# Causal mask of the third attention as triangles on quarters of TensorE, and its TensorE program without a loop

## The chip, the cores and the metric

The kernel runs on one core of one Trainium2 chip. The metric is the device time of one execution in microseconds (us). Three runs of the kernel before took 2063.49, 2064.55 and 2067.57 us, median 2064.55. Engines are TensorE (PE; its weight loads are PEld), VectorE (DVE), ScalarE (ACT), GpSimd (POOL) and SyncE, which issues the transfers (SPq).

## The reference

The reference is a stack of four layers on x of 16 samples x 256 tokens x 256 features, each an attention and a feed-forward part with a modulated layer norm in front and a gate behind: eight stages. The change touches the third stage, the attention of layer 1 (differential attention with 16 heads of two maps each, so 32 maps with 8 features):

```python
q = (x @ Wq).reshape(b, t, 2 * H, HD).transpose(0, 2, 1, 3) * scaling     # H = 16, HD = 8
k = (x @ Wk).reshape(b, t, 2 * H, HD).transpose(0, 2, 1, 3)
v = (x @ Wv).reshape(b, t, H, 2 * HD).transpose(0, 2, 1, 3)
scores = jnp.einsum('bhqd,bhkd->bhqk', q, k)
causal = jnp.triu(jnp.full((t, t), -jnp.inf, dtype=jnp.float32), 1)
aw = jax.nn.softmax((scores + causal).astype(jnp.float32), axis=-1)
aw = aw.reshape(b, H, 2, t, t)
aw = aw[:, :, 0] - lam * aw[:, :, 1]
attn = jnp.einsum('bhqk,bhkd->bhqd', aw, v)
attn = attn * jax.lax.rsqrt(jnp.mean(attn * attn, axis=-1, keepdims=True) + 1e-05)
attn = attn * (1.0 - LAMBDA_INIT)
return attn.transpose(0, 2, 1, 3).reshape(b, t, H * 2 * HD) @ Wo
```

## The kernel before

All of x stays in SBUF. Each engine has its own program, written by hand stage by stage (`l1a_tensor`, `l1a_vector`, `l1a_scalar`, `l1a_pool` and the `l1a_..._sync` functions for the third stage), and they meet by semaphores only. A stage's program is a function `slot(i)`, one per sample, called by the helper `slots`: some slots written out, the steady ones in a loop of two slots per turn (even and odd samples use different buffers), the last ones written out. For the third stage the loop covers slots 4 to 11 (`LOOP2`) on TensorE, VectorE, ScalarE and GpSimd. In the loop a semaphore's target is computed in a register.

In one slot TensorE interleaves three samples: the score maxima of sample i, most exponentials and the values of sample i - 1, the output of sample i - 2, and the projections of sample i + 1. The order is the one in `slot`.

Scores are computed twice. q and k are split in three bf16 parts each, and their products are six terms of eight features, 48 rows (`M_ROW`), stacked in QS and KS. `max_pair` computes scores with queries on the partitions, 48 rows deep, for two maps at once: map pr = 0 on rows 0 to 63 of the array, pr = 1 on rows 64 to 127, each into its own PSUM bank. VectorE takes the negated maximum over the keys (`maxima`, line 2322), GpSimd splits it in three bf16 parts, TensorE transposes them (`max_T`, line 2022), ScalarE copies them (`maxT`, line 2226) and SyncE writes them into QS (`l1a_max_sync`, line 2500), three rows behind the 48, against ones in KS. `exp_pair` then computes the scores again with keys on the partitions over 64 rows, now with the maximum taken off, and ScalarE takes the exponential straight from PSUM (line 2237). `values` multiplies by v (lines 2084, 2086), four heads on four 32-column tiles of the array.

A bank holds 512 columns. For each group of four heads (o = 0 to 3) there are three pairs (n = 0 to 2). Two of the three, here called short masks, hold two heads with 256 columns each, of which 128 need the mask; the third, the long mask, holds four heads with 128 columns, all masked (queries and keys of the same 128 tokens). The mask is a matmul too: the identity `ident_b` as weights over the whole array, a table of 0 and -1e30 (`later4` for the maxima, `earlier4` for the exponentials) as moving data. For short masks it comes behind the data (lines 2015, 2060), for long ones ahead of them (lines 2001, 2064). A sample has 24 pairs, 16 with a short and 8 with a long mask. Three banks turn round for the maxima and three for the exponentials: a pair waits until VectorE (`s.max`) or ScalarE (`s.prob`) has read the banks that it writes.

Work on the whole array (128 rows), on halves (64 rows, two side by side) and on 32-column tiles are three configurations of the array. The projections, transposes and masks use the whole one.

## Time and profile before

| | |
|---|---|
| median of the runs | 2064.55 us |
| profiled execution | 2068.32 us |
| its span, first to last instruction | 2066.5 us |
| TensorE busy, share of the span | 1837.7 us, 89% |
| VectorE | 1374.8 us, 67% |
| GpSimd | 901.9 us, 44% |
| ScalarE | 740.8 us, 36% |
| mean granted TensorE clock | 0.952 |
| chain that ended last, shares | TensorE 68%, VectorE 19%, issue 6% |

The third attention lies between 664.3 us (its first score matmul) and about 1226 us. TensorE's busy time is modelled: matmuls overlap in the array, so start-to-start distances are read rather than durations. A row with a bracket says how long the engine was idle ahead of it and what released it. Some matmul records are missing (a row x1 where two stand in the program).

### The profile page before, as it was taken

To read this page: it belongs to the slowest core of one execution; us is meant where nothing else is said; L and a number is where in the kernel's file an instruction comes from. 1 tells how busy PE (TensorE), PEld (TensorE's weight loads), DVE (VectorE), ACT (ScalarE), POOL (GpSimd) and SP (SyncE) were. 2 spreads that over 40 slices of the span, in tenths; PEclk is the share of its full clock that TensorE was granted. 3 is DMA by queue.
4 is the path that set the end of the run, shared out by engine and by line. 5 is a ranking of instruction groups with operands and counts; after the bars stand their busy time and mean duration, and the time that the engine had idled before them with its cause. 6 is when DMAs were issued, how large, how long until landed. Compare 5 with 4: busy or idle time off the path is not lost.

```text
span 2066.5 us, 39950 instructions
## 1 busy us (share of the span) xinstructions
PE 1837.7 (89%) x13335; PEld 1266.3 (61%) x13400; DVE 1374.8 (67%) x3587; ACT 740.8 (36%) x1511; POOL 901.9 (44%) x965
## 2 busy tenths in 40 slices
PE   8999999689997899999999988899867788998887
PEld 5555555489996455555555446677655667885443
DVE  4677767465554656565656567888846776886775
ACT  2544444122222464656464541111122223443332
POOL 0354545465555254545454443333343224663333
PEclk9999999799999899999999999999999888999787
DMA  5300000100004646454545400000011000000011
GB/s 181 106 6 8 5 8 6 35 6 10 9 10 95 138 84 112 84 109 81 109 81 111 79 7 14 8 10 8 15 32 41 13 16 16 16 13 18 31 38 41
DMA packets 68177, 93.34 MB, mean 45 GB/s; under 512 B 9852, under 2 KB 62316, under 8 KB 64748
## 3 DMA queue, kind: packets, MB, share of 16 engines
q1 hardware_dynamic: 68076, 92.01, 19.6%
q8 instruction: 61, 1.00, 0.2%
q14 instruction: 40, 0.33, 0.1%
HBM read 61.70 MB, written 29.49 MB: 44 GB/s over the span
## 4 chain that ended last, share of the span: by engine, by line
PE 68%; DVE 19%; issue 6%; POOL 2%; ACT 2%; DMA 1%; DVEq 1%; SPq 0%; POOLq 0%; ACTq 0%
PE PS L1029 16%; PE PS L2084 3%; PE PS L677 3%; DVE negmax L2322 3%; PE PS L1960 3%; PE PS L1196 3%; PE PS L734 3%; PE PS L750 2%; PE PS L510 2%; PE PS L2012 2%; DVE xn L500 2%; PE PS L2015 2%; PE PS L731 2%; PE PS L2057 2%; PE PS L701 1%
## 5 line engine op out<-in xcount | busy, mean ns | idle before, releaser
L2322 DVE TENSOR_REDUCE negmax<-PS 128x2 f32<-128x512 f32 (+1 forms) x384 | 247.1, 685 | 191.6 <-PE PS L2015 98.0
L541 POOL TENSOR_TENSOR X<-X,y_sb 128x512 f32 (+1 forms) x128 | 165.2, 1291 | 147.7 <-DVE y_sb L536 142.7
L536 DVE TENSOR_TENSOR y_sb<-PS,ga_sb 128x512 f32<-128x512 f32 x96 | 66.2, 690 | 180.3 <-PE PS L1029 50.4
L1029 PE MATMUL PS<-we_hi,h_parts 128*128 128x512 f32 x512 | 177.7, 407 | 1.6 <-POOL h_parts L1478 1.5
L500 DVE TENSOR_SCALAR xn<-X,mv,rs 128x256 f32 (+1 forms) x256 | 155.6, 649 | 22.5 <-POOL rs L493 21.2
L520 ACT ACTIVATE hT<-PS,modT 128x256 f32<-128x256 f32 x256 | 130.0, 559 | 112.5 <-PE PS L510 111.6
L2237 ACT ACTIVATE pw<-PS 128x512 f32<-128x512 f32 x256 | 139.0, 600 | 75.0 <-PE PS L2060 75.0
L491 POOL TENSOR_TENSOR rs<-mv,eps 128x2 f32<-128x2 f32 x128 | 26.6, 208 | 293.4 <-DVE mv L484 293.2
L1029 PE MATMUL PS<-l_h_parts,lut_hi 128*128 128x256 f32 (+1 forms) x768 | 145.7, 291 | 6.7 <-POOL l_h_parts L1162 6.7
L1029 PEld LDWEIGHTS PS<-l_h_parts,lut_hi 128*128 128x128 f32 (+1 forms) x768 | 117.8, 184 | 9.7 <-issue 5.4
L1572 DVE SCALAR_TENSOR_TENSOR l_acc<-PS,rt_g,l_acc 128x256 f32<-128x256 f32 x256 | 105.8, 475 | 20.8 <-PE PS L1029 20.7
L1029 PEld LDWEIGHTS PS<-we_hi,h_parts 128*128 128x128 f32 x512 | 96.8, 189 | 27.5 <-issue 7.1
L1029 PE MATMUL PS<-l_h_parts,lut_lo 128*128 128x256 f32 (+1 forms) x384 | 110.2, 287 | 0.0
L510 PE MATMUL PS<-ident,xn 128*128 128x128 f32 x512 | 82.1, 284 | 30.6 <-DVE xn L500 30.6
L1029 PE MATMUL PS<-we_lo,h_parts 128*128 128x512 f32 x256 | 101.9, 398 | 0.0
L1101 ACT ACTIVATE l0f_act<-PS 128x256 f32<-128x256 f32 x96 | 36.8, 383 | 176.4 <-PE PS L1029 176.4
L1196 PE MATMUL PS<-hT,l_wqkv 128*128 128x256 f32 x384 | 94.8, 399 | 5.1 <-ACT hT L520 4.3
L493 POOL TENSOR_TENSOR rs<-rs,half 128x2 f32<-128x2 f32 x128 | 94.1, 735 | 10.0
L1171 POOL TENSOR_TENSOR l0f_hid_parts<-l0f_hid,l0f_hid_parts 128x256 fp32r<-128x256 f32 x96 | 72.3, 754 | 53.2 <-DVE l0f_hid_parts L1023 52.7
L479 DVE BATCH_NORM_STATS2 st<-X 128x6 f32 (+1 forms) x256 | 95.1, 413 | 0.3
L510 PEld LDWEIGHTS PS<-ident,xn 128*128 128x128 f32 x512 | 58.7, 143 | 55.8 <-DVE xn L500 38.3
L997 POOL TENSOR_TENSOR l_ms<-l_ms,half 128x32 f32<-128x32 f32 x16 | 87.1, 5442 | 1.3
(279 smaller groups left out, 4372.3 us busy)
## 6 DMA issues: line engine op xcount, KB each, us to landing
ga_sb<-ga_dram SPq DMA_DIRECT2D x128, 128.0 KB, 2.9
qk_dram<-qk_parts SPq DMA_DIRECT2D x64, 192.0 KB, 2.8
KS<-qk_dram SPq DMA_DIRECT2D x32, 384.0 KB, 5.9
QS<-qk_dram SPq DMA_DIRECT2D x32, 384.0 KB, 9.3
qk_dram<-qk_parts SPq DMA_DIRECT2D x64, 128.0 KB, 2.8
wmod<-in_wmod SPq DMA_DIRECT2D x4, 1536.0 KB, 13.6
qk_dram<-qk_parts SPq DMA_DIRECT2D x64, 64.0 KB, 2.5
y_out<-X SPq DMA_DIRECT2D x16, 256.0 KB, 2.2
```

Source lines behind the costliest of these rows:

```text
L479: last_ = dve.bn_stats(st6[b.par][:, t, :], xb(b)[:, t, :])
L493: pool.tensor_tensor(rs[b.par][:, :], rs[b.par][:, :], half[:, 0:TT], ALU.pow).then_inc(s.rstd.sem, 1)
L500: last_ = dve.tensor_scalar(xn[b.par][:, t, :], xb(b)[:, t, :], mv[b.par][:, t, 0:1], rs[b.par][:, t:t + 1], ALU.subtract, ALU.mult)
L510: last_ = pe.transpose(PS[:, 0, kh * T + t * P:kh * T + (t + 1) * P], xn[b.par][:, t, kh * P:(kh + 1) * P], ident[:, :])
L520: last_ = act.activation(hT[b.par][:, kh, :], PS[:, 0, kh * T:(kh + 1) * T], ACT.Identity, bias=modT[:, sub, 0, kh, bass.ds(b.n, 1)], scal ...
L541: pool.tensor_tensor(xb(b), xb(b), y_sb[b.par][:, :, :], ALU.add).then_inc(s.x.sem, 1)
L997: pool.tensor_tensor(ms_sb[:, :], ms_sb[:, :], half[:, 0:TT * HEADS], ALU.pow).then_inc(s.rn.sem, 1)
L1029: last_ = pe.matmul(out, x.bitcast(F32R), y.bitcast(F32R), start=start and n == 0, stop=stop and n == 2)
L1196: last_ = pe.matmul(bank(1 + n)[:, m * T:(m + 1) * T], l3_wqkv[:, kh, n * D + m * P:n * D + (m + 1) * P], hT[b.par][:, kh, :], start=kh == ...
L1572: dve.scalar_tensor_tensor(l1_acc[b.par][:, t, :], bank(1 + (2 * q + t) % 4)[:, e * D:(e + 1) * D], rt_g[b.par][:, t, x_:x_ + 1], l1_acc[b ...
L2237: act.activation(to.rearrange("p a n -> p (a n)"), bank(4 + (2 * n + pr) % 3), ACT.Exp).then_inc(s.prob.sem, 1)
L2322: dve.tensor_reduce(to, src, AX.X, ALU.max, negate=True).then_inc(s.max.sem, 1)
```

## The change

Three things change, all for the third stage.

1. The mask. The upper right 128x128 mask splits in a 64x64 square that is masked altogether and two 64x64 triangles on the diagonal. The square goes into the data matmuls: two more rows in QS and KS (`S_ROW` is the old 48, `M_ROW` now 50), one per tile of 128 tokens, with 1 in the first 64 queries of the tile and -1e30 in its last 64 keys (`cut`). The triangles are added by `triangles`, four matmuls per pair with weights and data of 64x64: rows and columns 0 to 63 or 64 to 127 of the array, for bank 0 and bank 1 in turn. They now come behind the data in all pairs, and signal both banks in the second round.
2. `slots` can go without a loop, and TensorE's program of this stage is written out for all samples. The other engines keep their loop.
3. `l1a_cut_sync`: eight transfers that write the two rows, in the second stage (L0_ffn) at sample 14, and a wait for them at the start of TensorE's third stage.

```diff
 def slots(eng, slot, first, steady, last):
 
+    if steady is None:
+        steady = (first + first % 2,) * 2
     lo, hi = steady
-    assert lo % 2 == 0 and hi % 2 == 0 and hi > lo
+    assert lo % 2 == 0 and hi % 2 == 0 and hi >= lo
     for i in range(first, lo):
         slot(Idx(None, i))
-    with eng.Fori(lo // 2, hi // 2) as r:
-        slot(Idx(r * 2, 0))
-        slot(Idx(r * 2, 1))
+    if hi > lo:
+        with eng.Fori(lo // 2, hi // 2) as r:
+            slot(Idx(r * 2, 0))
+            slot(Idx(r * 2, 1))
...
+    cut_q, cut_k = np.zeros((2, HEADS, T), f), np.zeros((2, HEADS, T), f)
+    for t in range(TT):
+        cut_q[t, :, t * P:t * P + P // 2] = 1
+        cut_k[t, :, t * P + P // 2:(t + 1) * P] = LOW
+    out["cut"] = np.stack([cut_q, cut_k]).astype(bf)
...
+            pe.wait_ge(setup["a_pad"], 16 * 8)
...
+            def triangles(banks, tri, n, done):
+                for half_ in range(2):
+                    for pr in range(2):
+                        h = pr ^ half_
+                        r0, r1 = 64 * h, 64 * h + 64
+                        last_ = pe.matmul(banks[pr][r0:r1, :, r0:r1], ident_b[r0:r1, r0:r1], tri[r0:r1, 0:n, r0:r1],
+                                          start=False, stop=True)
+                        if half_ == 1:
+                            last_.then_inc(done.sem, 1)
...
                 if n == 0:
-                    for pr in range(2):
-                        pe.matmul(banks[pr], ident_b[:, :], later4[:, :, :], start=True, stop=False)
                     for j in range(4):
                         for pr in range(2):
-                            last_ = pe.matmul(banks[pr][:, j * P:(j + 1) * P], half_rows(q, pr, 4 * o + j, 0, P, M_ROW),
-                                              half_rows(k, pr, 4 * o + j, 0, P, M_ROW), start=False, stop=j == 3)
-                            if j == 3:
-                                last_.then_inc(s.max_ps.sem, 1)
+                            pe.matmul(banks[pr][:, j * P:(j + 1) * P], half_rows(q, pr, 4 * o + j, 0, P, M_ROW),
+                                      half_rows(k, pr, 4 * o + j, 0, P, M_ROW), start=j == 0, stop=False)
+                    triangles([x.rearrange("p (j k) -> p j k", j=4) for x in banks], later4, 4, s.max_ps)
                 else:
...
-                    for pr in range(2):
-                        pe.matmul(banks[pr].rearrange("p (j k) -> p j k", j=2)[:, :, P:T], ident_b[:, :], later4[:, 0:2, :],
-                                  start=False, stop=True).then_inc(s.max_ps.sem, 1)
+                    triangles([x.rearrange("p (j k) -> p j k", j=2)[:, :, P:T] for x in banks], later4, 2, s.max_ps)
...
-            slots(pe, slot, -2, LOOP2, B if pl + 1 < len(sigs) else B + 1)
+            slots(pe, slot, -2, None, B if pl + 1 < len(sigs) else B + 1)
...
-        M_ROW = 8 * N_TERMS
+        S_ROW = 8 * N_TERMS
+        M_ROW = S_ROW + TT
+
+
+        def l1a_cut_sync(sp):
+            sp.wait_ge(setup["a_zero"], 4)
+            for i in range(2):
+                for c, to in enumerate((QS, KS)):
+                    for r in range(2):
+                        sp.dma_start(to[i][64 * r + S_ROW:64 * r + M_ROW, :, :], ins["cut"][c]).then_inc(setup["a_pad"], 16)
...
-                    to = (QS, KS)[c][i.par][64 * r:64 * r + M_ROW, :, :].rearrange("p g t -> p (g t)")
+                    to = (QS, KS)[c][i.par][64 * r:64 * r + S_ROW, :, :].rearrange("p g t -> p (g t)")
...
+                    if i.reg is None and i.off == B - 2 and p == 1:
+                        l1a_cut_sync(sp)
```

`exp_pair` changes in the same way, with `earlier4`.

How TensorE's order moves is seen at the turn from one slot to the next, where it goes from the exponentials of one sample to the maxima of another, with the projection of k (`l_wk`) behind. Names are out<-moving data, weights, and the shape is that of the output. Before, outside the loop:

```order
L2057 MATMUL PS<-QS,KS 128x256 x4
L2060 MATMUL PS<-earlier,ident_b 128x2x128 x2
L2001 MATMUL PS<-later,ident_b 128x512 x2
L2004 MATMUL PS<-KS,QS 128x128 x8
L2064 MATMUL PS<-earlier,ident_b 128x512 x2
L2067 MATMUL PS<-QS,KS 128x128 x8
L1960 MATMUL PS<-hT,l_wk 128x256 x4
L2057 MATMUL PS<-QS,KS 128x256 x4
L2060 MATMUL PS<-earlier,ident_b 128x2x128 x2
L2012 MATMUL PS<-KS,QS 128x256 x4
L2015 MATMUL PS<-later,ident_b 128x2x128 x2
```

The same place of the changed kernel, with its own line numbers (2005 is `triangles`):

```order
L2073 MATMUL PS<-QS,KS 128x256 x4
L2005 MATMUL PS<-earlier,ident_b 64x2x64 x4
L2023 MATMUL PS<-KS,QS 128x128 x8
L2005 MATMUL PS<-later,ident_b 64x4x64 x4
L2079 MATMUL PS<-QS,KS 128x128 x8
L2005 MATMUL PS<-earlier,ident_b 64x4x64 x4
L1969 MATMUL PS<-hT,l_wk 128x256 x4
L2073 MATMUL PS<-QS,KS 128x256 x4
L2005 MATMUL PS<-earlier,ident_b 64x2x64 x4
L2030 MATMUL PS<-KS,QS 128x256 x4
L2005 MATMUL PS<-later,ident_b 64x2x64 x4
```

The long masks (512 columns, ahead of the data) stood next to other whole-array work and are now four triangles each behind the data. Short masks keep their place and become four triangles too.

In the loop of before TensorE's rows at the same turn have register instructions between them:

```order
L132 UNCONDITIONAL_BRANCH
L132 ISA
L1997 ISA
L2001 MATMUL PS<-later,ident_b 128x512 x2
L2004 MATMUL PS<-KS,QS 128x128 x8
L2045 REGISTER_ALU
L2064 MATMUL PS<-earlier,ident_b 128x512 x2
L2067 MATMUL PS<-QS,KS 128x128 x8
L1965 REGISTER_ALU
L1967 REGISTER_ALU
L1960 MATMUL PS<-hT,l_wk 128x256 x4
```

In the changed kernel this stage has none of them on TensorE. The last piece is SyncE's, at the end of the second stage: the gate loads of its samples 14 and 15, with the transfers of the two rows between, and the first transfer of the third stage. The changed kernel:

```order
L536 DMA ga_sb<-ga_dram 128x256
L2485 DMA QS<-in_cut 2x4096 x2
L2485 DMA KS<-in_cut 2x4096 x2
L2485 DMA QS<-in_cut 2x4096 x2
L2485 DMA KS<-in_cut 2x4096 x2
L536 DMA ga_sb<-ga_dram 128x256
L2496 DMA qk_dram<-qk_parts 64x3x512
```

The rows of `in_cut` stand there once for each of the two buffers; before, the two gate loads followed each other.

## Rows read from the trace of the kernel before

**Rows 1.** Busy us per stretch: from:to, length, PE, PEld, DVE, ACT, POOL, PEclk, DMA share, GB/s.

```profile
690.00:1190.00 500.00, 471.39 (x5148) 266.73 (x5206) 308.20 (x603) 279.44 (x547) 243.29 (x277) 1.00 0.51 99
748.36:783.17 34.81, 33.05 (x362) 18.85 (x365) 21.82 (x43) 19.39 (x38) 17.57 (x20) 1.00 0.52 95
817.98:852.78 34.80, 33.05 (x362) 18.85 (x365) 21.82 (x43) 19.47 (x38) 17.49 (x20) 1.00 0.53 100
```

**Rows 2.** TensorE in order of time: start us, length us, line, out<-in, rows*columns of the array.

```profile
836.00 0.39 PE L2057 MATMUL PS<-QS,KS 64*128 64x256 bf16 x4
836.32 0.39 PE L2060 MATMUL PS<-earlier,ident_b 128*128 128x256 bf16 x2
836.65 0.39 PE L2012 MATMUL PS<-KS,QS 48*128 48x256 bf16 x4
...
840.41 0.39 PE L2060 MATMUL PS<-earlier,ident_b 128*128 128x256 bf16 x2
840.64 0.59 PE L2001 MATMUL PS<-later,ident_b 128*128 128x512 bf16 x2
841.17 0.40 PE L2004 MATMUL PS<-KS,QS 48*128 48x128 bf16 x8
```

**Rows 3.** TensorE in order of time, eighth stage: 8, 64 and 72 columns.

```profile
1886.79 1.03 PE L1765 MATMUL PS<-hT,l_m 128*8 128x256 f32 x4
1887.75 1.08 PE L1719 MATMUL PS<-hT,l_sw 128*64 128x256 f32 x4
1888.76 1.08 PE L1721 MATMUL PS<-hT,l_up 128*72 128x256 f32 x4
```

**Rows 4.** TensorE in order of time, second stage: from 128 to 48 columns.

```profile
618.99 0.28 PE L1029 MATMUL PS<-l_h_parts,lut_lo 128*128 128x256 f32 x1
619.11 0.40 PE L1029 MATMUL PS<-l_h_parts,lut_hi 128*48 128x256 f32 x2
```

**Rows 5.** Groups by line: busy us, mean ns of one, idle us before; weight load of 64 columns.

```profile
L1719 PEld LDWEIGHTS PS<-hT,l_sw 128*64 128x64 f32 x64 | 7.7, 142 | 13.1 <-issue 8.1 <-DVE l_c L1815 2.0 <-ACT hT L520 0.4
```

**Rows 6.** Weight loads in order of time, first stage: strips of 32 rows.

```profile
208.56 0.31 PEld L731 LDWEIGHTS PS<-l_qT,l_kT 32*128 32x128 f32 x8 [0.33 <-issue]
```

**Rows 7.** Waits of SyncE's queue, 440 to 640 us: us in total, times, longest.

```profile
SPq L528 <- DVE y_sb L536: 182.2, 13, 21.7
```

**Rows 8.** TensorE in order of time, with its waits for VectorE.

```profile
848.91 0.39 PE L2012 MATMUL PS<-KS,QS 48*128 48x256 bf16 x4
...
850.30 0.39 PE L2012 MATMUL PS<-KS,QS 48*128 48x256 bf16 x4 [0.68 <-DVE negmax L2322]
...
859.40 0.39 PE L2012 MATMUL PS<-KS,QS 48*128 48x256 bf16 x4 [0.32 <-DVE negmax L2322]
```

**Rows 9.** VectorE in order of time.

```profile
858.66 2.67 DVE L2322 TENSOR_REDUCE negmax<-PS 128x2 f32<-128x512 f32 x4
```

**Rows 10.** ScalarE in order of time.

```profile
836.64 1.08 ACT L2237 ACTIVATE pw<-PS 128x512 f32<-128x512 f32 x2
```

**Rows 11.** TensorE in order of time: transpose of the maxima, and their use.

```profile
863.65 0.28 PE L2022 MATMUL PS<-ident_b,mparts 128*128 128x128 bf16 x2
...
868.07 0.39 PE L2057 MATMUL PS<-QS,KS 64*128 64x256 bf16 x4
```

**Rows 12.** TensorE in order of time, the same in the last sample.

```profile
1176.93 0.29 PE L2022 MATMUL PS<-ident_b,mparts 128*128 128x128 bf16 x2
...
1181.03 0.39 PE L2057 MATMUL PS<-QS,KS 64*128 64x256 bf16 x4 [1.54 <-DMA QS<-maxT]
...
1182.65 1.08 PE L2084 MATMUL PS<-pw,l_vpad 128*32 128x256 f32 x8
...
1185.34 0.39 PE L2057 MATMUL PS<-QS,KS 64*128 64x256 bf16 x4
```

**Rows 13.** Transfers issued from 829 to 864 us: KB each, median us to landing.

```profile
QS<-qk_dram SPq DMA_DIRECT2D x2, 384.0 KB, 9.9
```

**Rows 14.** SyncE's queue in order of time.

```profile
852.35 0.88 SPq L2489 DMA_DIRECT2D QS<-qk_dram  x2
```

More of the change, by code:

```diff
@@ L2058, in exp_pair @@
                                       half_rows(q, pr, g, 0, T, 64), start=j == 0, stop=False)
-                    for pr in range(2):
-                        pe.matmul(banks[pr].rearrange("p (j q) -> p j q", j=2)[:, :, 0:P], ident_b[:, :], earlier4[:, 0:2, :],
-                                  start=False, stop=True).then_inc(s.score.sem, 1)
-                else:
-                    for pr in range(2):
-                        pe.matmul(banks[pr], ident_b[:, :], earlier4[:, :, :], start=True, stop=False)
+                    triangles([x.rearrange("p (j q) -> p j q", j=2)[:, :, 0:P] for x in banks], earlier4, 2, s.score)
+                else:
                     for j in range(4):
                         for pr in range(2):
-                            last_ = pe.matmul(banks[pr][:, j * P:(j + 1) * P], half_rows(k, pr, 4 * o + j, P, T, 64),
-                                              half_rows(q, pr, 4 * o + j, P, T, 64), start=False, stop=j == 3)
-                            if j == 3:
-                                last_.then_inc(s.score.sem, 1)
+                            pe.matmul(banks[pr][:, j * P:(j + 1) * P], half_rows(k, pr, 4 * o + j, P, T, 64),
+                                      half_rows(q, pr, 4 * o + j, P, T, 64), start=j == 0, stop=False)
+                    triangles([x.rearrange("p (j q) -> p j q", j=4) for x in banks], earlier4, 4, s.score)
             def values(b, o):
```

## The prediction

> **What bounds the kernel now.** I read the stages first (busy time of each engine in stretches), then the order of time inside the third attention, the one stage that is changed, then who waits there. In the 500 us of its steady part TensorE is busy 471 us at the full clock, VectorE 308, ScalarE 279, GpSimd 243, and the DMA engines half of the time [rows 1]. Cut at ScalarE's eviction of the values, which comes once a sample, a sample takes 34.8 us [rows 1]. So the stage is TensorE's, with short stretches in which it waits for another engine.
>
> **What a mask costs.** A score pair is some data matmuls on two halves of the array (64 rows each, side by side) and a mask on the whole array. From start to start the four data matmuls of 256 columns take 0.32 us (836.00 to 836.32), the two masks of 256 columns 0.33 (836.32 to 836.65), and the two masks of 512 columns 0.53 (840.64 to 841.17) [rows 2]. So 512 more mask columns cost 0.21, two masks of 256 stream for 0.21, and 0.11 is left: the price of going from whole array to halves. Halves to whole costs the same (0.32 less two rounds of 0.107). Where a whole-array mask follows whole-array work there is no such price: 840.41 to 840.64 is 0.23 [rows 2].
>
> **The change, part by part.**
> (a) Stream. The mask of 128x128 becomes four triangles of 64x64: two rounds of 128 columns for the short mask (0.107 us in place of 0.213), two rounds of 256 for the long one (0.213 in place of 0.427), if the quarters run side by side as the halves do. A sample has 16 short and 8 long masks: 16 x 0.107 + 8 x 0.213 = 3.4 us.
> (b) Switches. The long mask came first, often right behind whole-array work, as the order rows show. Now each of the 24 pairs is halves, then quarters. Changes of configuration counted through one sample: 50 before, 60 now; 10 x 0.11 = 1.1 us more, if halves to quarters costs 0.11 too. No row has this switch. The nearest keep all rows and change the columns: from 8 to 64 columns costs 1887.75 - 1886.79 - 4 x 0.213 = 0.11, from 64 to 72 columns 0.16 [rows 3]; 128 to 48 columns costs nothing, as the step of 0.12 stays (618.99 to 619.11) [rows 4]. Bounds 0 and 0.16; I take 0.11, the row whose matmuls end at 64 columns. The Trainium skill (TensorEngine Tiling (Array Packing), Tiling Modes, Key Properties) says that changing the tiling mode, unlike changing the tile, drains TensorE: a rule against this change. By it all 60 cost, and the sum is mine; the row at 619.11 does not agree, and by that row the 24 inner ones are free, which is rival 1.
> (c) Weights. Each triangle loads 64 columns of the identity: four loads where there were two. A load of 64 columns in f32 lasts 142 ns [rows 5]; I take no more for bf16. Loads overlap where they go to different rows: eight, to four row strips, stand in 0.31 us [rows 6], where even one of half its columns lasts 0.14. The triangles go to two different halves of the rows, so I take no cost; the other bound is that each load holds up the next, which makes a short mask as long as before (rival 3). The Trainium skill (TensorE: Matmul & The Clock Gate, Part 2) gives the quick weight load to 128 columns only and otherwise P / 1.2 ns for P columns: an estimate of 53 ns, four in a row 0.21, which would be rival 3. No row here has a bf16 load of 64 columns.
> (d) The data matmuls of the maxima get two more rows (48 to 50) and no more columns, and those of the exponentials always had 64 rows at the same 0.32. Nothing.
> (e) The program without the loop. One sample stands outside the loop (748.36 to 783.17), one in it (817.98 to 852.78): 34.81 and 34.80 us, TensorE busy 33.05 in both [rows 1]. So the loop costs nothing now, and writing it out gives nothing. Below zero: more code to fetch, which the sample outside had too. Above: register instructions before waits could begin to count once pairs are shorter, and are gone.
> (f) Eight small transfers on SyncE's queue, late in the second stage, at about 0.44 us of issue each (0.88 for two, [rows 14]): 3.5 us, ahead of one gate load. That queue waits 182 us for VectorE there, over 13 loads [rows 7]. Hidden; without that cover one gate load would be 3.5 us late, once.
>
> **What TensorE gets to keep.** Its work falls by 3.4 - 1.1 = 2.3 us a sample, but in six stretches another engine sets the length.
> VectorE, three times. From 848.91 to 850.30, 1.39 us, are data, switch, one mask, a maximum of 0.69 and the hand-over: none gets shorter, since the first of two masks in a row was as long as two rounds of triangles [rows 8]. The stretch before it (L2012 at 845.00) has the same 1.39. And up to 859.40, from the last transpose to tokens on, VectorE runs without a pause (its maxima from 858.66 on have no idle time ahead), and TensorE waits 0.32 for it [rows 8, 9]. These hold 5 short masks and 1 of the new switches.
> ScalarE, three times. The pair that starts at 836.00 has its first exponential at 836.64, which ends 0.6 later; with the hand-over the next exponential pair cannot start before 1.3 us have gone [rows 10]. TensorE's own two pairs there take 2 x 0.65 now, 2 x 0.54 after. The same holds seven microseconds later, and behind the transpose at 863.65, where two evictions stand ahead on ScalarE. These hold 5 short masks, 1 long, 3 new switches.
> Left: 6 x 0.107 + 7 x 0.213 = 2.13 us, less 6 x 0.11 = 0.66: 1.47.
> Then a new wait. The negated maxima go through a transpose on TensorE, ScalarE, and SyncE's transfer, before the third group's exponentials. TensorE has 863.65 to 868.07, 4.42 us, between transpose and use [rows 11]; in the last sample, where a projection between them is missing, it waited 1.54 us and used them 4.10 after (1176.93 to 1181.03) [rows 12]. After: 4.42 - 0.53 + 0.11 = 4.0, a wait of 0.1; behind it in TensorE's order stands everything. The big loads of Q and K land 9.9 us after their issue at 852.35 to 853.23, by 863.1, and are used from about 864.4; that comes 1.3 earlier at most, and their own issue moves too: nothing [rows 13, 14].
> Kept: 1.47 - 0.1 = 1.35 us a sample. The steady part from 683 to 1181 us is 14.3 samples: 19 us. The first sample (maxima alone, VectorE's) and the last (exponentials alone, ScalarE's) give nothing.
> The profiled execution took 2068.3 us for a span of 2066.5; less 19 it is 2049. The median of the runs shown lies 3.8 lower, at 2064.55: I forecast 2046.
>
> **Rivals.**
> 1. Halves to quarters is free. For it the row at 619.11, against it [rows 3]. The 13 pairs outside the set stretches gain 0.11 more each, 1.4 us: 2.75 a sample, 39 us, 2025.
> 2. Slower: the quarters don't run side by side, in all 24 masks of a sample. The triangles stream 0.213 and 0.427 as before, the 6 switches (0.66) stay as pure cost, and in the VectorE and ScalarE stretches the banks come up to 0.1 later: 0.9 more a sample, 13 us, 2077. It decides once a short mask streams over 0.17. For it: no row has two tiles that differ in rows and columns both; against: halves do run side by side.
> 3. The four weight loads follow one another: a short mask stays 0.21, a long one gets 0.21. 7 x 0.213 = 1.49, less 0.66, less 0.1 for the maxima, less 0.5 in the set stretches, where both masks come 0.1 later: 0.2 a sample, 3 us, 2062. Against it [rows 6].
> 4. Behind the wait of 1.54 the clock was low, and the values took 2.69 us (1182.65 to 1185.34) [rows 12], half of which they need at the full clock. If the new waits did this in each sample, 1.3 would eat the gain: 2064. Against it: waits of 0.68 in each sample leave the clock at 1.00 [rows 1, 8].
> That the change doesn't do what it says can only be its second half, and (e) says that.
>
> **Chances and range.** Forecast 0.50, rival 1 0.16, rival 2 0.12, rival 3 0.12, rival 4 0.04, something unnamed 0.06 spread over all. A measurement of this kernel tells about 0.2%, 4 us, from no change. Faster 0.73 (forecast, rival 1, a part of rival 3), same 0.13, slower 0.14. The forecast's own range, with the switch at 0.09 to 0.13, is 2036 to 2054. To 2024 the range takes in rival 1, to 2070 rivals 3 and 4 and the near part of 2.
>
> **What would show it.** The sample's 34.81 us become 33.3 to 33.6. From the first short triangle to the next data matmul 0.22 (0.32: loads one after another, or not side by side); from data to triangles 0.32 (0.21: the switch is free). TensorE still waits for VectorE at three places, longest at the third; a wait of about 0.1 for the maxima's transfer and waits for ScalarE before exponential pairs appear. Clock 1.00 from 690 to 1170. The forecast is wrong if the sample's step is over 34.2 or under 32.8, or if another stage moves by more than 3 us.

## The result, and the profile after

The changed kernel takes 2040.46 us (median of 4 runs, 2036.71 to 2046.87), the kernel before 2064.02 (median of 4, 2063.12 to 2067.57). The ratio is 0.9882, with a 95% interval of 0.9862 to 0.9901: faster by 23.6 us. The forecast was 2046, in a range of 2024 to 2070.

The stage that is changed, in the trace after: busy us per stretch, in the columns of [rows 1].

```profile
804.93:838.40 33.47, 31.48 (x414) 19.09 (x413) 21.93 (x43) 19.51 (x38) 17.48 (x20) 1.00 0.51 101
690.00:1160.00 470.00, 438.01 (x5774) 264.74 (x5776) 307.18 (x598) 272.96 (x533) 240.76 (x275) 1.00 0.53 104
```

A sample takes 33.47 us where it took 34.81, with the clock at 1.00. TensorE is busy 1.6 us less than the 33.05 of [rows 1], with 52 more matmul records: 48 triangles, and 4 that the trace of before lacks. Against the complete records of the same masks (33.47, shown below for the kernel before without its loop) it is 2.0 us less, where 2.3 were forecast. The other three engines do what they did.

TensorE in order of time in the same trace: start us, length us, line, out<-in, rows*columns of the array.

```profile
848.88 0.28 PE L2038 MATMUL PS<-ident_b,mparts 128*128 128x128 bf16 x2
849.10 0.39 PE L2073 MATMUL PS<-QS,KS 64*128 64x256 bf16 x4
849.42 0.30 PE L2005 MATMUL PS<-earlier,ident_b 64*64 64x128 bf16 x4
849.66 0.40 PE L2023 MATMUL PS<-KS,QS 50*128 50x128 bf16 x8
849.98 0.41 PE L2005 MATMUL PS<-later,ident_b 64*64 64x256 bf16 x4
850.49 0.40 PE L2079 MATMUL PS<-QS,KS 64*128 64x128 bf16 x8
850.82 0.41 PE L2005 MATMUL PS<-earlier,ident_b 64*64 64x256 bf16 x4
851.15 1.99 PE L1969 MATMUL PS<-hT,l_wk 128*128 128x256 f32 x8
853.08 0.39 PE L2073 MATMUL PS<-QS,KS 64*128 64x256 bf16 x4
```

Data to triangles is 0.32 (849.10 to 849.42), of which 0.21 is stream; a short mask to the next data 0.24; a long mask to the next matmuls 0.33 (850.82 to 851.15), about 0.10 more than the short one for 512 more columns spread over four matmuls. What TensorE waited for in the sample from 804.93 to 838.40 (total us, times, longest), first its matmuls, then its weight loads:

```profile
PE PS L2030 <- DVE negmax L2333: 1.2, 2, 0.8
PE PS L2023 <- DVE negmax L2333: 0.2, 1, 0.2
```

```profile
PEld PS L2079 <- ACT pw L2248: 1.0, 3, 0.4
PEld PS L2073 <- ACT pw L2248: 0.5, 2, 0.3
PEld PS L2073 <- ACT pz L2248: 0.3, 1, 0.3
```

VectorE holds TensorE's matmuls at three places, and ScalarE its weight loads at six.

**Where the time came from.** GpSimd adds to x once a sample, 16 times a stage. I compare the stretch between its thirteenth addition of the second stage and its first of the fourth, which holds the third stage and a little of both neighbours. These two additions in the trace after:

```profile
605.68 1.30 POOL L549 TENSOR_TENSOR X<-X,y_sb 128x512 f32 x1 [2.94 <-DVE y_sb L544]
1232.90 1.30 POOL L549 TENSOR_TENSOR X<-X,y_sb 128x512 f32<-128x512 f32 x1
```

That is 627.2 us, and 651.4 in the kernel before (612.66 to 1264.02): 24.1 less. From the last addition of the second stage to the last of the third it is 575.3 (645.34 to 1220.61) and 599.4 (652.29 to 1251.70), again 24.1 less. Twelve steady samples give 16.2 (401.54 us against 417.70 between the same evictions), the two samples ahead of them 2.0 and 1.4, and the end of the stage 4.6. In the profiled executions 7.5 us more went elsewhere, 6.2 of them in the first 90 us, where the code is the same: the same 32 small matmuls took 7.01 us in one execution and 4.05 in the other. The median moved by 23.6, close to the stage's 24.1, so those 7.5 are put down to the two executions and not to the change.

### The profile page after: what moved, and what is told of

It reads as the page before. It is cut to its first block, busy times and chain, and to the rows that moved or that the text cites. A ratio compares the mean times of both kernels' runs of the same rounds, so it can differ in the third digit from the quotient of the medians.

```text
span 2034.9 us, 41282 instructions
## 1 busy us (share of the span) xinstructions
PE 1804.3 (89%) x14168; PEld 1264.1 (62%) x14168; DVE 1374.9 (68%) x3587; ACT 742.3 (36%) x1511; POOL 902.2 (44%) x965
## 4 chain that ended last, share of the span: by engine, by line
PE 64%; DVE 20%; issue 7%; ACT 4%; POOL 2%; DMA 1%; DVEq 1%; SPq 0%; ACTq 0%; POOLq 0%
PE PS L1037 16%; PE PS L2005 4%; PE PS L685 3%; PE PS L742 3%; DVE negmax L2333 3%; PE PS L1969 3%; PE PS L1204 3%; PE PS L2095 3%; PE PS L758 2%; DVE xn L508 2%; PE PS L518 2%; PE PS L739 2%; ACT pw L2248 2%; PE PS L2030 2%; PE PS L709 2%
```

## The experiments

All are compared by the steady step (one sample, from eviction to eviction, as in [rows 1]) and by the length of the third stage, which in the table is the stretch between additions as just defined. Both are read inside one execution, so what differs at its head doesn't enter. A single execution's whole time varies by 5 us and more, and the kernel before, run beside each group of experiments, took 2061.1 to 2066.5.

| kernel | steady step | third stage | whole |
|---|---|---|---|
| before | 34.81 | 651.4 | 2064.0 |
| before, TensorE's loop written out | 34.80 | 651.4 | 2061.8 |
| before, loop, masks cut in two | 35.17, three of 43 | 679.6 | 2096.6 |
| changed | 33.47 | 627.2 | 2040.5 |
| changed, with the loop | 33.47, three of 42 | 655.8 | 2062.8 |
| triangles in the exponentials alone, loop | 34.03 | 639.2 | 2052.5 |
| triangles, one quarter a round | 33.53 | 636.2 | 2045.7 |
| triangles, one row half | 33.46 and 34.83 | 649.4 | 2064.6 |
| triangles, one quarter only | 35.88 | 679.9 | 2090.5 |
| whole masks on halves | 33.61 | 632.4 | 2045.9 |
| triangles on halves | 31.39 | 599.8 | 2010.5 |
| no triangles | 30.7 mean | 587.7 | 2001.1 |

The whole times of the changed kernel, of the kernel before and of triangles on halves are medians; all else is one execution each. The step is the median of the twelve steady samples, where the table gives one number and no mean. The stage's length also holds its start and end, where the clock goes to its lower level for a longer or a shorter time: in the kernel before 34.1 us in all, in the changed one 30.7, with one quarter a round 51.2. A difference of a few us in the stage that the steady samples don't show therefore tells nothing by itself.

### The two halves of the change, each alone

The changed kernel with TensorE's loop put back:

```diff
-            slots(pe, slot, -2, None, B if pl + 1 < len(sigs) else B + 1)
+            slots(pe, slot, -2, LOOP2, B if pl + 1 < len(sigs) else B + 1)
```

> The changed kernel with TensorE's loop over pairs of samples put back; the triangles stay. Compared by the steady step of the third stage (ScalarE's eviction of the values, once a sample), 33.47 us in the changed kernel. My theory: the loop costs nothing, so 33.4 to 33.5 in the samples of the loop too, and TensorE's waits stay as they are. Rival: with shorter pairs the register instructions of the loop begin to count: over 33.6 inside the loop, and 33.47 only in the samples outside it.

Measured: both theories were wrong. The ordinary samples take 33.47, but three take 41.67, 41.77 and 41.39: every second one between 836 and 1028 us, and the loop of samples 4 to 11 goes back three times. One ordinary sample and one of the three, in the columns of [rows 1]:

```profile
802.88:836.35 33.47, 31.48 (x414) 19.09 (x413) 21.94 (x43) 19.51 (x38) 17.48 (x20) 1.00 0.51 98
836.35:878.02 41.67, 33.88 (x414) 20.47 (x413) 21.89 (x43) 19.51 (x38) 17.52 (x20) 0.92 0.44 85
```

TensorE has two long gaps in the long sample, both put down to "issue": no semaphore and no engine that the trace knows held it. In order of time:

```profile
847.38 0.30 PE L2005 MATMUL PS<-earlier,ident_b 64*64 64x128 bf16 x4
850.51 0.40 PE L2023 MATMUL PS<-KS,QS 50*128 50x128 bf16 x8 [2.83 <-issue]
850.84 0.41 PE L2005 MATMUL PS<-later,ident_b 64*64 64x256 bf16 x3
854.31 0.42 PE L2005 MATMUL PS<-later,ident_b 64*64 64x256 bf16 x1 [3.07 <-issue]
```

And the stretch around the second one and behind it:

```profile
852.00:859.00 7.00, 4.69 (x21) 3.17 (x21) 0.69 (x1) 1.09 (x2) 0.78 (x2) 0.51 0.02 5
```

The second gap comes in the middle of a group of four triangles, where the program has no wait. Two gaps make 5.9 us of the 8.2. The clock, at its lower level (1.2 GHz) from a little after 852 to about 859, makes most of the rest: the K projection, 1.93 us from start to start otherwise, took 3.46. Three times 8.2, 8.3 and 7.9 are 24.4 us, all that the triangles bring.

The other half alone, TensorE's program written out and the masks as before:

```diff
-            slots(pe, slot, -2, LOOP2, B if pl + 1 < len(sigs) else B + 1)
+            slots(pe, slot, -2, None, B if pl + 1 < len(sigs) else B + 1)
```

> The kernel before with only TensorE's program of the third attention written out without a loop; its masks are as before. My theory: this half of the change is worth nothing, the steady step stays 34.8 us and the time 2064 within 4 us. Rival: unrolling carries part of the gain at the start and the end of the stage (the first samples gave 3.5 us and the end 4.5, which I had put at nothing): then a part of that shows here.

Measured: 34.80 us a sample, the third stage 651.4, as long as in the kernel before. Written out, the trace has 366 matmul and 365 weight load records in a sample; [rows 1] has 362 matmuls for the same code, since a few records are missing there.

```profile
814.61:849.41 34.80, 33.47 (x366) 18.85 (x365) 21.81 (x43) 19.46 (x38) 17.50 (x20) 1.00 0.50 98
```

So neither half makes the stage shorter alone (655.8 and 651.4 against 651.4), and both together make it 24.1 shorter.

### Is it the length of the loop's body?

The kernel before with its loop, and each mask matmul cut in two:

```diff
-                    for pr in range(2):
-                        pe.matmul(banks[pr], ident_b[:, :], later4[:, :, :], start=True, stop=False)
+                    for c in range(2):
+                        for pr in range(2):
+                            pe.matmul(banks[pr][:, c * T:(c + 1) * T], ident_b[:, :], later4[:, 2 * c:2 * c + 2, :], start=c == 0, stop=False)
...
```

> The kernel before, with its loop, whole masks and order, and each mask matmul cut in two of half the columns: the same columns streamed, and as many TensorE instructions in the loop's body as in the changed kernel with a loop (where each of the loop's three ways back cost 8 us: two gaps of 3 us in which nothing held TensorE but issue, then a low clock). My theory: the size of the body is the cause (the target of the branch is fetched anew once the body is too long), so the ways back cost 8 us here as well, 24 in all, and the other samples take 34.8 to 35.5 us: 2090. Rival: triangles or their order make the gaps; here none, and 2064 to 2072.

Measured: three long samples at the three ways back (42.91, 43.71, 43.09; 24.2 us over the 35.17 of the others), with no triangle in the kernel.

```profile
816.36:851.52 35.16, 33.79 (x414) 21.84 (x413) 21.81 (x43) 19.60 (x38) 17.49 (x20) 1.00 0.51 98
851.52:894.43 42.91, 36.68 (x414) 23.27 (x413) 21.90 (x43) 19.61 (x38) 17.48 (x20) 0.92 0.41 79
```

Each long sample has two gaps put down to "issue" again, 2.7 and 2.2 us in this one.

The changed kernel with the loop, and the kernel before's masks in the 12 pairs of the maxima:

```diff
-                    triangles([x.rearrange("p (j k) -> p j k", j=2)[:, :, P:T] for x in banks], later4, 2, s.max_ps)
+                    for pr in range(2):
+                        pe.matmul(banks[pr].rearrange("p (j k) -> p j k", j=2)[:, :, P:T], ident_b[:, :], later4[:, 0:2, :],
+                                  start=False, stop=True).then_inc(s.max_ps.sem, 1)
...
```

> The changed kernel with TensorE's loop, and triangles only in the 12 pairs of the exponentials; the maxima have the masks and the order of the kernel before. The loop's body lies halfway between that of the kernel before (no gap at the ways back) and that of the changed kernel with a loop (8 us at each). Theory, threshold above the middle: no gap, step about 34.2 us, 2055. Threshold below: three gaps of 8 us, 2079. Either way the other samples show what the exponentials' half of the triangles is worth: 0.5 to 0.9 of the 1.35 us, since the stretches set by ScalarE lie there.

Measured: no gap, all steady samples 34.00 to 34.04.

```profile
846.87:880.90 34.03, 32.49 (x390) 18.91 (x389) 21.81 (x43) 19.50 (x38) 17.45 (x20) 1.00 0.51 97
```

By the matmul and weight load records of two samples, a body of 1462 (kernel before) and one of 1558 go back free; at 1654 each way back costs 8 us, whether triangles or cut masks fill it. To these come about 90 register, branch and waiting instructions in each of these bodies. The Trainium skill (Runtime: NRT & Kernel Launch, Instruction fetch mechanics) says that instructions come in blocks by a transfer of their own, ahead of their use, and that a taken branch whose target is no longer at hand waits for it. The trace agrees with the mechanism, at 2.2 to 3.3 us a gap and two gaps a way back. The same section of the Trainium skill gives TensorE room for 2048 instructions; here the limit lies lower, between 1558 and 1654 records and the ninety beside them. No run shows the fetch itself beside the gap, so that it is the fetch is inferred from the body's length alone. Where the body lies in the program was not varied apart from its length.

The exponentials' half of the triangles is worth 0.78 us of the 1.34.

### Do quarters run side by side?

Both maps of a round on one quarter:

```diff
-                        h = pr ^ half_
+                        h = half_
```

> The changed kernel with one edit: both maps of a round of triangles go to the same quarter of the array (first the upper left, then the lower right), where the change sends them to different ones. Columns, weight loads, waits and result are the same. My theory: the gain of the change is that two quarters stream side by side; here a short mask streams 0.213 us and a long one 0.427, as whole masks did, and the steady step becomes 35.5 to 35.9 us, about 0.9 over the kernel before. Rival: the gain comes from the order (data first, mask last) and from smaller masks as such, and the place doesn't matter: 33.5.

Measured: my forecast of this run was wrong. The step is 33.53, 0.06 over the changed kernel, and a long mask to the next matmuls takes 0.33 or 0.34 as before. The rounds are not barriers: the second round, on the other quarter, could start beside the first. The stage is 8.9 us longer than in the changed kernel, but only 0.8 of them lie in the twelve steady samples; the others are at its start and end, where the lower clock lasts 20.5 us longer. So I went on, first to one row half:

```diff
-                        last_ = pe.matmul(banks[pr][r0:r1, :, r0:r1], ident_b[r0:r1, r0:r1], tri[r0:r1, 0:n, r0:r1],
+                        last_ = pe.matmul(banks[pr][r0:r1, :, r0:r1], ident_b[0:64, 0:64], tri[0:64, 0:n, 0:64],
```

> The changed kernel with all four triangles of a pair computed by rows 0 to 63 of the array (the same triangle and the same part of the identity; the outputs go where they went). With both maps of a round on one quarter, the step was 33.53 us, where I had forecast 35.5 to 35.9: the two rounds still used both row halves, one after the other in the program. My theory now: what runs side by side are the two row halves, whatever the order within four triangles; on one row half nothing does, a short mask streams 0.213 and a long one 0.427, from short triangles to the next data 0.33 us (0.23 in the changed kernel), step 35.3 to 35.9 us. Rival: the triangles' time isn't their stream (weight loads or the change of configuration set it): 33.5 here too.

Measured: wrong again. The masks cost the same: 0.23 and 0.33 from their start to the next matmuls.

```profile
956.08 0.30 PE L2005 MATMUL PS<-earlier,ident_b 64*64 64x128 bf16 x4
956.31 0.39 PE L2030 MATMUL PS<-KS,QS 50*128 50x256 bf16 x4
...
958.97 0.41 PE L2005 MATMUL PS<-earlier,ident_b 64*64 64x256 bf16 x4
959.30 1.04 PE L518 MATMUL PS<-ident,xn 128*128 128x128 f32 x4
```

Every second sample, though, takes 34.83, and not by the masks: the clock falls to its lower level at 959.4 and comes back at 962.8. The two kinds of sample:

```profile
918.11:951.57 33.46, 31.48 (x414) 19.10 (x413) 22.00 (x43) 19.50 (x38) 17.45 (x20) 1.00 0.51 102
951.57:986.40 34.83, 32.94 (x414) 19.71 (x413) 21.81 (x43) 19.72 (x38) 17.48 (x20) 0.95 0.48 94
```

Then all four triangles on the one quarter of rows and columns 0 to 63. The triangles overwrite scores here in place of masking them, and the last data matmuls close their bank, which the diff leaves out (neither was tried by itself):

```diff
-                        last_ = pe.matmul(banks[pr][r0:r1, :, r0:r1], ident_b[r0:r1, r0:r1], tri[r0:r1, 0:n, r0:r1],
-                                          start=False, stop=True)
+                        last_ = pe.matmul(banks[pr][0:64, :, r0:r1], ident_b[0:64, 0:64], tri[0:64, 0:n, 0:64],
+                                          start=True, stop=True)
```

> The changed kernel with all four triangles of a pair on one quarter of the array (rows 0 to 63, columns 0 to 63): as many matmuls and columns, but they overwrite a part of the scores in place of masking it, so the output is not the reference's. On one quarter per round, and on one row half, the samples at the full clock kept 33.5 us. My theory: quarters do run side by side, by rows and by columns both, and the matmuls queue for each quarter apart, so that both earlier edits still had two of them at work; here nothing is left to run beside, a long mask streams 0.427 us (0.53 to 0.55 from its start to the next matmuls, 0.33 in the changed kernel), a short one 0.33, and the step is 35.3 to 35.9 us. Rival: a matmul of 64 rows and 64 columns streams in half its columns' time by itself, and side by side has nothing to do with it: 0.33, 0.23 and 33.5 here too.

Measured: as forecast. A short mask takes 0.34 and a long one 0.55 to the next matmuls, and every steady sample 35.88 or 35.89.

```profile
860.05 0.41 PE L2005 MATMUL PS<-earlier,ident_b 64*64 64x128 bf16 x4
860.39 0.39 PE L2030 MATMUL PS<-KS,QS 50*128 50x256 bf16 x4
...
863.05 0.62 PE L2005 MATMUL PS<-earlier,ident_b 64*64 64x256 bf16 x4
863.60 0.66 PE L518 MATMUL PS<-ident,xn 128*128 128x128 f32 x4
```

So quarters do run side by side, and it does not matter how: with different rows and columns, with the same rows, or with two matmuls in a row for one quarter and two for another. For the last, the single matmuls in the trace show the way. With one quarter a round, the program's order is twice the upper left quarter, then twice the lower right, and only the last two signal a semaphore. In the trace a signalling one starts 0.007 us behind the first, and the other matmul of the first quarter only 0.13 behind (850.110, 850.117, 850.243, 850.250); the order is the same in all 333 groups of four between 680 and 1150 us. So a matmul that waits for its quarter doesn't hold up the next one for another quarter. With nothing side by side the step is 2.41 us longer, and 1.07 longer than in the kernel before: the slower rival of the prediction, priced at 0.9. The four weight loads alone don't explain this, since a long mask has as many loads as a short one, and takes 0.21 more than it here, 0.10 more in the changed kernel.

### What the changes of configuration cost

The triangles on halves of the array, 64 rows by 128 columns like the data, with a shifted identity as weights:

```diff
+    mid = np.zeros((P, 192), f)
+    mid[k, 64 + k % 64] = 1
+    out["mid"] = mid.astype(bf)
...
-                        h = pr ^ half_
-                        r0, r1 = 64 * h, 64 * h + 64
-                        last_ = pe.matmul(banks[pr][r0:r1, :, r0:r1], ident_b[r0:r1, r0:r1], tri[r0:r1, 0:n, r0:r1],
-                                          start=False, stop=True)
+                        r0, r1 = 64 * pr, 64 * pr + 64
+                        c0, c1 = 64 * half_, 64 * half_ + 64
+                        last_ = pe.matmul(banks[pr][:, :, c0:c1], mid[r0:r1, 64 - c0:192 - c0], tri[r0:r1, 0:n, r0:r1],
+                                          start=False, stop=half_ == 1)
```

> The changed kernel with each triangle on a half of the array in place of a quarter: 64 rows by 128 columns, by the weights of a shifted identity (a constant of 128x192 of which a window is taken; 64 columns of it are zero, so it adds zeros to the other rows of the bank). As many triangles, columns and waits as in the changed kernel, but the configuration of the data matmuls is kept, so that a sample has 22 changes of configuration in place of 60. My theory: each change costs 0.11 us on TensorE, some of it hidden where VectorE or ScalarE set the length; the steady step goes from 33.47 to 31.6 us (-1.9; up to 38 x 0.11 = 4.2 if nothing else held it), the kernel to 2013 us (2005 to 2022), and a wait for the transfer of the stacks of Q and K, 0.3 to 0.8 us a sample, appears. Rival: what looks like a change of configuration is the load of the first 64-column weights after a data matmul, or the drain of a bank; then the 0.32 from data to mask stays, the step is 33.4 and the kernel 2040.

Measured: 2010.50 us (median of 4, 2008.17 to 2016.60) against 2066.49 of the kernel before beside it, ratio 0.9732 (0.9707 to 0.9757), clear of the changed kernel's interval. The median step is 31.39, the mean of the twelve 31.56.

```profile
924.80:956.20 31.40, 28.23 (x414) 19.90 (x413) 21.80 (x43) 19.31 (x39) 17.88 (x20) 1.00 0.54 107
```

```profile
928.87 0.39 PE L2077 MATMUL PS<-QS,KS 64*128 64x256 bf16 x4
929.10 0.28 PE L2009 MATMUL PS<-earlier,mid 64*128 64x128 bf16 x4
...
931.43 0.28 PE L2009 MATMUL PS<-later,mid 64*128 64x128 bf16 x4
931.54 0.39 PE L2083 MATMUL PS<-QS,KS 64*128 64x128 bf16 x8
```

Data to mask 0.23 in place of 0.32, a short mask to the next data 0.11 in place of 0.23. What TensorE's matmuls waited for in that sample, of other engines and transfers:

```profile
PE PS L2034 <- DVE negmax L2337: 1.4, 2, 0.8
PE PS L2083 <- ACT pw L2252: 0.9, 2, 0.4
PE PS L2027 <- DMA QS<-qk_dram: 0.4, 1, 0.4
PE PS L2027 <- DVE negmax L2337: 0.2, 1, 0.2
```

The stack of Q, which landed in time so far, is now late by 0.4, as expected. 38 changes fewer make 2.08 us (1.9 by the mean); at 0.11 each TensorE's own share would be 4.2, so about half of it is lost to the other engines.

The rival has two parts. A drain of the bank is out, since banks and order stayed. The load of 64-column weights is not tested by this run alone, since `mid` has 128 columns. But the masks of the kernel before have 128-column weights too, and data to mask takes 0.32 there as well (836.00 to 836.32 [rows 2]). In both kernels the mask's weight load starts with its matmul (836.319 and 836.323, 849.424 and 849.425); here it starts 0.107 ahead of it (928.993 and 929.100), while the data still stream. So the price goes with the configuration, and what it costs is the overlap of the next weight load with the stream.

Whole masks of 128x128 on halves, without the cut by constant rows. The diff is against the kernel with triangles on halves, and leaves out the tables, which are laid out anew for two halves:

```diff
-                        last_ = pe.matmul(banks[pr][:, :, c0:c1], mid[r0:r1, 64 - c0:192 - c0], tri[r0:r1, 0:n, r0:r1],
+                        last_ = pe.matmul(banks[pr], mid[r0:r1, 64 - c0:192 - c0], tri[r0:r1, half_, 0:n, :],
...
-        M_ROW = S_ROW + TT
+        M_ROW = S_ROW
```

> Whole masks of 128x128 as in the kernel before (no cut by constant rows, none of their transfers), but computed on two halves of the array (64 rows each, shifted identity), behind the data and without a loop. Streams as before (0.213 and 0.427 us), 22 changes of configuration a sample in place of 50. My theory, from the step of 31.4 us with triangles on halves: here 3.4 us more stream, of which VectorE's and ScalarE's stretches take a part: 33.4 to 33.8 us, about 1.2 less than before; so the configurations alone are worth nearly what the triangles were. Rival: the gain on halves needs the short masks: 34.8.

Measured: 33.61, and 632.4 for the stage.

```profile
874.96:908.58 33.62, 31.37 (x414) 20.41 (x413) 22.10 (x43) 19.40 (x38) 17.47 (x20) 1.00 0.53 105
```

The two levers stand beside each other: 28 changes fewer than before give 1.20 at an unchanged stream; triangles on top of that give 2.22. (The 1.20 also holds two things not tried apart: long masks now stand behind the data, and each mask is four matmuls in place of two, which by itself cost 0.36 above, 35.17 against 34.81.) The changed kernel pulled the second and pushed the first the wrong way (10 changes more), and kept 1.34 of their 3.42.

Last, the changed kernel without the triangles (the mask within each 64x64 block on the diagonal is left out), to see what the other engines allow:

```diff
             def triangles(banks, tri, n, done):
+                return
...
-                                      half_rows(k, pr, 4 * o + j, 0, P, M_ROW), start=j == 0, stop=False)
+                                      half_rows(k, pr, 4 * o + j, 0, P, M_ROW), start=j == 0, stop=j == 3)
```

> The changed kernel without the triangles (the mask inside each 64x64 block on the diagonal is left out, and its time with it). The triangles stand for 24 x 2 changes of configuration and for 3.4 us of stream a sample, 8.7 us of TensorE in all (24 x 2 x 0.11 + 3.4). My theory: the stretches set by VectorE and ScalarE keep a good part of this: step 29.8 to 30.6 us, with waits for VectorE and ScalarE of 3 us and more a sample and a wait for the transfer of the stacks. Rival: TensorE gets it all back: 24.8 us; or the stacks' transfer sets the pace from 31.4 on, where it first shows with 0.4: 31.0 or more.

Measured: 30.7 us on the mean of 13 samples (700.81 to 1099.57), uneven from 29.5 to 32.3, the clock at 0.97 over them; just above my range. The forecast had put 48 changes of configuration on the triangles; counted in the trace they are 38 (60 less 22), and this work would be 7.6 us and not 8.7. A sample at the full clock, and its waits:

```profile
916.54:946.42 29.88, 24.59 (x318) 16.23 (x317) 22.04 (x43) 19.16 (x39) 17.81 (x20) 1.00 0.57 111
```

```profile
PE PS L2033 <- DVE negmax L2342: 1.9, 3, 0.9
PE PS L2086 <- ACT pw L2257: 1.5, 2, 0.8
PE PS L2024 <- DMA QS<-qk_dram: 1.1, 1, 1.1
```

TensorE's 6.9 us less work than in the changed kernel (24.59 against 31.48) is worth 3.6 in such a sample. The stage is 12 us shorter than with triangles on halves (587.7 and 599.8). As it ran, a better mask could gain no more than this; but the clock was at its lower level for 20.5 us of the twelve steady samples here and never there, so this is no firm bound.

## Why the prediction was right, and where it wasn't

**The sum.** The step was forecast to fall by 1.35 us to 33.3 to 33.6; it fell by 1.34 to 33.47.

**(a) Stream.** Right: 0.10 between a long and a short mask's way to the next matmuls, and 2.41 us a sample once nothing runs beside a triangle. My picture of it was too narrow: I thought that the two of a round must differ in rows and columns both. The two runs in between show that they need not.

**(b) Switches.** Right in size: halves to quarters costs 0.09 to 0.11 (data to mask 0.32, against 0.23 on halves or 0.21 of stream), near the value taken from the row at 1887.75 [rows 3] and not the free one [rows 4]. The rule of the Trainium skill that was weighed there (TensorEngine Tiling (Array Packing), Tiling Modes, Key Properties) holds for this switch: without it data to mask takes 0.23 in place of 0.32. So rival 1, the free switch, is out.

**(c) Weights.** Right: four short triangles and the switch behind them take 0.23, which leaves 0.12 for all four loads and streams together. Rival 3 would have shown 0.32.

**(d), (f) The two constant rows and their transfers.** Right as far as it shows: the maxima's data matmuls, now 50 rows, keep 0.32 (849.66 to 849.98), and the second stage, with the eight transfers issued from 605.90 us on, doesn't take longer: from the addition ahead of them to the last of the stage it is 39.7 us (605.68 to 645.34), and 39.6 before (612.66 to 652.29).

**(e) The program without the loop.** This step failed. "So the loop costs nothing now, and writing it out gives nothing" is true of the kernel before (34.80, 651.4) and false of the change: it is what keeps the triangles' gain. With the loop the third stage is 28.6 us longer (655.8 against 627.2). 24.4 of them are the three ways back; the other 4 or so lie at its start and end, where the lower clock lasts 10.2 us longer, and one execution doesn't tell whether the loop does that. I had named two effects that could speak for or against it, code to fetch and register instructions, and compared a sample in the loop with one outside, for a body that the change was about to lengthen from 1462 to 1654 records. That the number came out right is luck here: both halves were in the kernel, and a forecast of the triangles alone from the same sum would have missed the 24 us of the ways back.

**What TensorE gets to keep.** The waits fit the six stretches, which were not tried one by one. VectorE waits are at the three places (0.8, 0.4, 0.2). ScalarE now holds pairs as said: 1.39 from 849.10 to 850.49, and 1.8 us of waits before weight loads in a sample, against 1.1 before. The work fell by 2.0 us and the step by 1.34. The wait of 0.1 for the maxima's transfer did not come: between the transpose and the use lie 4.20 us (848.88 to 853.08), not 4.0, probably because ScalarE's hold of the pair at 850.49 lies on that way and fills it.

**Start and end.** The mis-sized term is here: 19 us for the stage, measured 24.1. The stage's first step between evictions stayed (41.97 and 41.96), the second fell by 2.0 (31.74 to 29.75), where VectorE was to hold it, and the end by 4.6. Of the 2.0 the clock has 0.5 or so: in the kernel before its lower level reaches 1.3 us into this step, and in its version without the loop, where it hardly does, the step is 31.26. At the end, too, part of it is the clock. Behind the wait of 1.54 [rows 12] the kernel before has this stretch, then the changed kernel the same place behind its own wait of 1.66:

```profile
1182.00:1186.00 4.00, 4.00 (x44) 1.76 (x42) 1.29 (x2) 1.27 (x4) 0.00 (x0) 0.59 0.00 1
```

```profile
1154.04 0.39 PE L2073 MATMUL PS<-QS,KS 64*128 64x256 bf16 x4 [1.66 <-DMA QS<-maxT]
```

```profile
1153.00:1157.00 4.00, 2.96 (x56) 1.64 (x56) 1.29 (x2) 1.86 (x5) 2.06 (x1) 1.00 0.11 36
```

The wait is longer by 0.12 and the clock stays. That belongs to rival 4, with its sign turned round: a wait as long as that does not by itself lower the clock, and I had no row that told me when it does. Behind the last eviction the clock stands at its lower level for 13.7 us in the kernel before and for 10.2 in the changed one. At half speed these 3.4 us are worth 1.7 at most, so at least 2.9 of the 4.6 are something else; which waits became shorter there stays open.

**Signs of being wrong.** No other stage moved by more than 3 us, but for the first, and there it is the 6.2 us of its head, which differ between executions of the same code.

## What to carry to other kernels

An edit that adds instructions to a looped program has a second price, which no comparison of samples before the edit shows: count the body, and look at the samples in which the loop goes back, not at a median one. Look at how often the array's configuration changes before shortening what runs in it; a zero-padded weight that keeps the configuration gave more here (2.08 us a sample) than the triangles themselves kept (1.34). And before taking an experiment as a test of "side by side", make sure that really nothing is left to run beside: two of three edits here left something.

## What the runs showed of the hardware that I had not expected

- A way back in TensorE's loop is free at 1462 and 1558 records a body and costs 7.7 to 8.5 us at 1654, as two gaps of 2.2 to 3.3 us and a half clock behind them.
- Quarters of the array run side by side also when they share their rows (33.46 us a sample), and when two matmuls in a row go to the same quarter and the next two to another (33.53), against 35.88 with one quarter alone. In the second case matmuls start out of the program's order: the third 0.007 us behind the first, the second 0.13 behind it.
- At the step from data to mask, behind a change of configuration, the weight load starts with its matmul; without the change it starts 0.107 us ahead of it. The step takes 0.32 and 0.23 us.
- In the one execution with all triangles on rows 0 to 63, the clock goes to its lower level for some 3 us in every second sample (34.83 us). With all triangles on one quarter, rows 0 to 63 too, it stays at 1.00 in all twelve steady samples (35.88), as it does with triangles on both row halves. So it is not the rows alone, and no run shows what lowers it.
